# State-space stage of a four-layer kernel: another order of the engines' jobs, the first row's softplus sums and skip inputs dealt out, the bias prepared ahead

## The reference

```python
x = x + mamba(layernorm(x))      # the state-space stage: the change is here
x = x + experts(layernorm(x))    # 8 experts, the best 2 for each token, capacity 80 a row
x = x + attention(layernorm(x))  # causal, one head
x = x + experts(layernorm(x))
```

```python
xc, z = split(x @ in_proj_w + in_proj_b)
xc = silu(conv4(xc) + conv_b)                      # causal, per channel
delta_s, B, u = split(xc @ x_proj_w + x_proj_b)    # 16, 16, 512
delta = softplus(delta_s @ dt_proj_w + dt_proj_b)
h[t] = exp(-delta[t] * n) * h[t-1] + delta[t] * B[t, n] * u[t]    # n = 1..16
y = sum over n of h + u * D
out = (y * silu(z)) @ out_proj_w + out_proj_b
```

## Time and profile before

| | us |
|---|---|
| median of 3 runs | 2976.49 |
| the profiled execution | 2975.88 |
| its span | 2974.1 |
| first scan starts | 57.5 |
| last scan starts | 1620.0 |
| turn 1 (first scan of row 0 to that of row 1) | 97.3 |
| turn 2 | 97.0 |
| turns 3 to 14 | 98.2 to 99.4 |

### The profile page before, as it was taken

One profiled execution on the slowest core, in us unless ns is written; L12 is line 12 of the kernel. 1 busy time (PEld: TensorE's weight loads), 2 busy tenths in 40 slices (PEclk: granted clock), 3 DMA queues, 4 the chain that ended last, 5 costly groups with the idle time before them and its releaser, 6 DMA issues. The chain is left out here.

```text
span 2974.1 us, 48729 instructions
## 1 busy us (share of the span) xinstructions
PE 2760.2 (93%) x16944; PEld 2222.7 (75%) x16944; DVE 2274.6 (76%) x3610; ACT 1757.6 (59%) x3174; POOL 2190.4 (74%) x1437
## 2 busy tenths in 40 slices
PE   6999999999999899999986799999899997999998
PEld 3566656666666566656665799999898987999998
DVE  4898999999999998999888656565477775656564
ACT  4766776677667766776664445454366654544443
POOL 4889899899989999989987666666335557666664
PEclk9999999999999999999998899999999997999999
DMA  6132221122112211221125455545222234454542
GB/s 171 69 110 74 88 72 32 74 88 72 38 67 88 72 46 59 88 74 44 52 81 197 133 120 123 121 124 117 60 76 80 91 107 123 125 120 121 123 117 37
DMA packets 184191, 273.01 MB, mean 92 GB/s; under 512 B 35687, under 2 KB 156174, under 8 KB 175816
## 3 DMA queue, kind: packets, MB, share of 16 engines
q1 hardware_dynamic: 148680, 227.92, 23.2%
q0 software_dynamic: 35328, 42.76, 8.0%
HBM read 188.89 MB, written 94.72 MB: 95 GB/s over the span
## 5 line engine op out<-in xcount | busy, mean ns | idle before, releaser
L550 POOL TENSOR_TENSOR dbu<-du,bb 128x1024 f32<-128x1024 f32 x512 | 1196.8, 2365 | 27.4 <-DVE hs L703 24.2
L703 DVE TENSOR_TENSOR_SCAN hs<-da,dbu 128x1024 f32<-128x1024 f32 x512 | 1152.9, 2280 | 67.6 <-ACT da L638 29.0
L638 ACT ACTIVATE da<-delta 128x512 f32<-128x512 f32 x1024 | 567.9, 594 | 238.4 <-DVE hs L703 235.8
L808 PEld LDWEIGHTS yT<-ident,hs 128*128 128x128 f32 x4096 | 483.6, 146 | 142.3 <-issue 99.7
L808 PE MATMUL yT<-ident,hs 128*128 128x128 f32 x4096 | 540.2, 282 | 14.6 <-DVE hs L703 14.6
L1365 POOL TENSOR_TENSOR ffn_w_lo<-ffn_w,ffn_w_hi 128x512 fp32r<-128x512 f32 x240 | 320.7, 1339 | 80.3 <-ACT ffn_w_hi L1360 78.6
L1449 PE MATMUL ffn_hbank<-ffn_w_hi,ffn_hT_hi 128*128 128x256 f32 x1280 | 367.2, 287 | 0.3 <-DVE ffn_hT_lo L1436 0.3
L1451 PE MATMUL ffn_hbank<-ffn_w_hi,ffn_hT_lo 128*128 128x256 f32 x1280 | 360.2, 281 | 0.0
L1450 PE MATMUL ffn_hbank<-ffn_w_lo,ffn_hT_hi 128*128 128x256 f32 x1280 | 360.1, 281 | 0.0
L1414 PE MATMUL ffn_hbank<-ffn_rowsT_hi,ffn_w_hi 128*128 128x320 f32 x1024 | 318.5, 311 | 3.2 <-POOL ffn_w_lo L1365 3.2
L1415 PE MATMUL ffn_hbank<-ffn_rowsT_lo,ffn_w_hi 128*128 128x320 f32 x1024 | 318.1, 311 | 0.0
(11 more groups left out here) (260 smaller groups left out, 4957.3 us busy)
## 6 DMA issues: line engine op xcount, KB each, us to landing
bb<-b_rows SPq DMA_DIRECT2D x64, 1024.0 KB, 4.6
ffn_w<-L_ffn_W SPq DMA_DIRECT2D x60, 1024.0 KB, 6.2
slots<-empty SPq DMA_DIRECT2D x40, 530.0 KB, 8.2
empty<-slots SPq DMA_DIRECT2D x16, 662.5 KB, 4.9
ffn_rows<-slots SPq DMA_DIRECT2D x16, 662.5 KB, 4.8
xt<-L_attn_a_x SPq DMA_DIRECT2D x16, 512.0 KB, 3.9
x<-L_attn_a_x SPq DMA_DIRECT2D x16, 512.0 KB, 3.9
x_after_mamba<-x SPq DMA_DIRECT2D x16, 512.0 KB, 3.0
```

The lines of the kernel that those rows point to most:

```text
L550: pool.tensor_tensor(dbu[:, s % DEEP], du[:, dt, :].unsqueeze(1).to_broadcast([P, SN, T]), bb[:, q * SN:(q + 1) * SN, :], ALU.mult).then_i ...
L638: ins = act.activation(da[:, s % 2, i, :], delta[:, par, dt, :], ACT.Exp, scale=-float(q * SN + i + 1))
L703: dve.tensor_tensor_scan(flat[0], flat[1], flat[2], 0.0, ALU.mult, ALU.add).then_inc(scanned.sem, 1)
L808: mm = pe.matmul(yT[:, j * P:(j + 1) * P], hs[:, s % DEEP, i, j * P:(j + 1) * P], k.ident[:], start=False, stop=(q == QS - 1 and i == SN - ...
```

## The change

The job orders of all engines are written anew, and with them the step under which each job stands. The bank orders change too, so other pairs of jobs share a bank. Beside the order:

- log_part of row 0 is split: block 0 first, with a semaphore of its own (log_begun), then blocks 1 to 3. The softplus sums 1 to 3 of row 0, its step_input 1 and 2 and its skip_input 0 to 2 move from the end of turn 0 into the steps 0 to 5 of turn 1. The normalisation of row 1 moves from step 30 of turn 0 to step 1 of turn 1.
- stage_bias moves from step 0 of turn 1 to step 10 of turn 0.
- prompt_stats of the next row moves from step 13, behind gate 0, to step 12.
- route_place moves ahead of gate 2 in step 31.

```diff
-RING_JOBS = ("G3", "Z0", "U2", "O0", "T0", "T1", "U3", "I0", "I1", "O1", "G0", "Z1", "I2", "I3", "S", "RT0", "RT1",
-             "DA0", "DA1", "DA2", "DA3", "G1", "RL", "U0", "Z2", "U1", "G2", "RP", "Z3", "-")
+RING_JOBS = ("G3", "Z0", "U2", "O0", "T0", "T1", "U3", "I0", "O1", "I1", "G0", "I2", "Z1", "I3", "RT0", "S",
+             "RT1", "DA0", "DA1", "DA2", "DA3", "-", "RL", "G1", "U0", "Z2", "U1", "G2", "RP", "Z3")
...
         def softplus(pool, row, par, m):
-            pool.wait_ge(log_done.sem, log_done.at(row, 1))
+            if is_turn(row, 0) and m == 0:
+                pool.wait_ge(log_begun, 1)
+            else:
+                pool.wait_ge(log_done.sem, log_done.at(row, 1))
...
             act.wait_ge(exp_done.sem, exp_done.at(row, 2))
-            act.activation(tail_of_xc, tail_of_xc, ACT.Ln, bias=1.0).then_inc(log_done.sem, 1)
+            if is_turn(row, 0):
+                act.activation(tail_of_xc[:, 0, :], tail_of_xc[:, 0, :], ACT.Ln, bias=1.0).then_inc(log_begun, 1)
+                act.activation(tail_of_xc[:, 1:, :], tail_of_xc[:, 1:, :], ACT.Ln, bias=1.0).then_inc(log_done.sem, 1)
+            else:
+                act.activation(tail_of_xc, tail_of_xc, ACT.Ln, bias=1.0).then_inc(log_done.sem, 1)
... POOL
+                        if s == 1 and is_turn(turn, 1):
+                            softplus(pool, 0, 0, 1)
+                        if s == 3 and is_turn(turn, 1):
+                            softplus(pool, 0, 0, 2)
+                        if s == 5 and is_turn(turn, 1):
+                            softplus(pool, 0, 0, 3)
...
-                        if s == 30 and has_first(turn):
+                        if s == 27 and has_first(turn) and turn > 0:
                             softplus(pool, turn, par, 1)
+                        if s == 28 and has_first(turn) and turn > 0:
                             softplus(pool, turn, par, 2)
-                        if s == 31 and has_first(turn):
+                        if s == 30 and has_first(turn) and turn > 0:
                             softplus(pool, turn, par, 3)
... ACT
+                        if s == 0 and late:
+                            summed_copy(act, turn, turn - 2, 3)
                         if s == 1 and late:
                             gate_input(act, turn, 3)
-                            summed_copy(act, turn, turn - 2, 3)
...
-                        if s == 6 and first:
+                        if s == 4 and first:
                             for c in range(NC):
                                 turned(act, turn, par, c)
...
+                        if s == 26 and main:
+                            summed_copy(act, turn, row, 2)
+                        if s == 26 and first and turn > 0:
+                            skip_input(act, turn, turn, 0)
... DVE
-                        if s == 0 and is_turn(turn, 1):
-                            stage_bias(dve)
+                        if s == 1 and is_turn(turn, 1):
+                            step_input(dve, 0, 0, 0, 1)
...
-                        if s == 5 and main:
+                        if s == 6 and main:
                             step_input(dve, turn, row, 1 - par, 3)
                         if s == 10 and is_turn(turn, 0):
                             dve.wait_ge(loaded, 16 * CONSTS)
                             dve.tensor_tensor(b_skip[:], b_u[:], d_skip[:], ALU.mult).then_inc(skip_ready, 1)
                             dve.wait_ge(k.shaped, KIT_SHAPED)
+                            stage_bias(dve)
...
+                        if s == 12 and has_first(turn + 1):
+                            dve.wait_ge(x_ld.sem, x_ld.at(turn + 1, 16))
+                            prompt_stats(dve, norm, xt, turn + 1)
                         if s == 13 and main:
                             gate(dve, turn, 0)
-                        if s == 13 and has_first(turn + 1):
-                            dve.wait_ge(x_ld.sem, x_ld.at(turn + 1, 16))
-                            prompt_stats(dve, norm, xt, turn + 1)
                         if s == 13 and late:
                             route_stats(dve, turn, turn - 2)
...
-                        if s == 31 and first:
+                        if s == 29 and first and turn > 0:
                             step_input(dve, turn, turn, par, 1)
+                        if s == 31 and late:
+                            route_place(dve, turn, turn - 2)
                         if s == 31 and main:
                             gate(dve, turn, 2)
-                        if s == 31 and late:
-                            route_place(dve, turn, turn - 2)
... PE
                         if s == 3 and main:
                             x_proj(pe, turn, 3, 0)
+                        if s == 3 and first:
+                            in_proj(pe, turn, par, "I0", 0)
+                        if s == 4 and main:
                             x_proj(pe, turn, 3, 1)
...
                             dt_proj(pe, turn, 2)
-                        if s == 18 and first:
                             dt_proj(pe, turn, 3)
...
                             x_proj(pe, turn, 0, 0)
+                        if s == 23 and first:
                             x_proj(pe, turn, 0, 1)
...
-                        if s == 30 and main:
+                        if s == 31 and main:
                             in_proj(pe, turn, 1 - par, "Z3", ND + 3)
```

More of the change, by code:

```diff
@@ L972, in one_turn @@
                             summed_copy(act, turn, row, 0)
-                        if s == 9 and first:
+                        if s == 11 and first:
                             conv_input(act, turn, 1)
@@ L994, in one_turn @@
                             act.wait_ge(skip_ready, 1)
+                        if s == 19 and late:
+                            route_turned(act, turn, 1)
                         if s == 19 and main:
                             summed_copy(act, turn, row, 1)
-                        if s == 19 and first:
+                        if s == 20 and first:
                             delta_b(act, turn)
-                        if s == 19 and late:
-                            route_turned(act, turn, 1)
                         if s == 21 and first:
@@ L1118, in one_turn @@
                             pe.wait_ge(staged, STAGED)
+                        if s == 0 and late:
+                            out_proj(pe, turn, 0)
+                        if s == 1 and first:
+                            turn_x(pe, turn, 0)
                         if s == 1 and late:
-                            out_proj(pe, turn, 0)
                             out_proj(pe, turn, 1)
-                        if s == 2 and first:
-                            turn_x(pe, turn, 0)
                         if s == 3 and first:
@@ L1127, in one_turn @@
                             x_proj(pe, turn, 3, 0)
+                        if s == 3 and first:
+                            in_proj(pe, turn, par, "I0", 0)
+                        if s == 4 and main:
                             x_proj(pe, turn, 3, 1)
-                        if s == 4 and first:
-                            in_proj(pe, turn, par, "I0", 0)
-                        if s == 6 and first:
+                        if s == 6 and late:
+                            out_proj(pe, turn, 2)
@@ L1132, in one_turn @@
+                        if s == 7 and first:
                             in_proj(pe, turn, par, "I1", 1)
-                        if s == 7 and late:
-                            out_proj(pe, turn, 2)
                         if s == 8 and first:
                             conv_taps(pe, turn, 0)
-                            conv_taps(pe, turn, 1)
                         if s == 8 and late:
                             out_proj(pe, turn, 3)
+                        if s == 8 and first:
+                            conv_taps(pe, turn, 1)
@@ L1140, in one_turn @@
                         if s == 9 and main:
                             turn_back(pe, turn, row, 0)
+                        if s == 9 and first:
+                            in_proj(pe, turn, par, "I2", 2)
                         if s == 10 and main:
                             in_proj(pe, turn, 1 - par, "Z1", ND + 1)
-                        if s == 10 and first:
-                            in_proj(pe, turn, par, "I2", 2)
+                        if s == 11 and is_turn(turn, 0):
+                            pe.wait_ge(loaded, 16 * CONSTS)
@@ L1155, in one_turn @@
                             route_turn(pe, turn, turn - 2, 0)
-                        if s == 14 and late:
+                        if s == 13 and first:
+                            x_proj_small(pe, turn, 0)
+                        if s == 15 and late:
                             route_turn(pe, turn, turn - 2, 1)
```

94 lines of the change are left out of this document (50 added, 44 removed).

## The result

The kernel after takes 3013.35 us (median of 4 runs, 3012.37 to 3013.49) against 2975.59 of the kernel before: ratio 1.0124, 95% interval 1.0109 to 1.0139. It is slower, as forecast, but by 37.8 us and not by 21. The 2997 of the forecast was missed by 16 us, and the range, which ended at 3007, by 6.

The account below looks back on a forecast made before the run. Steady turns were taken as set by waits between engines, POOL pacing the first 29.3 us and DVE the rest. Terms -10.9 + 2 - 2.0 + 31.8 - 0.3 + 0.7 = +21.3 gave 2997 us; full range 2961 to 3007.

Parts of the forecast that it names:

- The sign and the first mechanism: Whole kernel slower, +21.3 us (slower 0.62): in steady turns norm_veps or norm_away loses the port until POOL's product 16 ends.
- Rival 1: Steady turns: norm_veps and norm_away both run between POOL products 15 and 16, +0.35 a turn; 2968 us, chance 0.22.
- rivals 2 and 4: 2: norm_veps' wait stays 0.4, turn gains 0.8, 2953, chance 0.07; 4: order costs nothing, start gives nothing, 2973, 0.08.
- The statistics of the next row: Turns 3 to 14: statistics at step 12 lose the port, scan 14 +2.95; with -0.3, +2.65 a turn, +31.8 in all.
- End of a turn: Steady turns, up to the routing's end: earlier yT copy and reordered gate 2, U0 and DA3; -0.3 a turn, bounds -1.0 to +1.0.
- The start: Row 0: split logarithm and U0's new bank bring the first scan from 57.52 to near 51.8; -5.7 us, bounds -1.5 to -6.5.
- The bias: Row 0: its DVE work between the first scans moves to idle time in turn 0; -6.2 us, 1 put back for softplus sums.
- the wait in turn 1: Turn 1: the same port wait costs about 3 us, of which 1 had been waited for anyway; +2 us.
- Turn 2: DVE's 3.06 us wait for U3 shrinks through earlier queueing and an earlier yT copy; -2.0 us, bounds 0 to -3.
- The tail: Turn 17: Z3 behind the last sum delays silu and gate 3 by 1.5, out_proj 2 gains 0.8; +0.7 us.
- Rival 3: Steady turns: scan 22 behind DA3, or xnT copies before decay 5, add 1 us each on top; +13, 3010 us, chance 0.08.

Follow-up runs that it names:

- kernel 2: Kernel after, with the next row's statistics put back behind gate 0 (step 13): 3003.84 us against 3023.75 for the kernel before, ratio 0.9945.
- kernel 1: Kernel before, with only the next row's statistics moved to step 12, ahead of gate 0: 3085.01 us against 3023.75, ratio 1.021.
- kernel 5: Kernel after, with the next row's statistics in step 13 but still ahead of gate 0: mean of turns 3 to 14 is 98.46 us (one run).
- the last kernel of part 7: Kernel after, with norm_veps and norm_away on POOL and Z3 at step 29, ahead of sum 30: 2961.14 us against 2976.72 for the kernel before.
- kernel 8: Kernel after, with norm_veps and norm_away on POOL and gate 0 in step 12 ahead of the statistics: 2946.91 us against 2976.77 for the kernel before.
- last kernel of part 5: Kernel after, with gate 0 moved to step 12, ahead of the statistics: 2989.40 us against 2976.77 for the kernel before, ratio 1.0040.

## Why the prediction was right and wrong

- *The sign and the first mechanism: right.* The place, step 12, and the way in which the port is lost were called: norm_veps in front of a boundary of queued products, ending only with product 16. It was norm_veps itself that lost it, so scan 14 came 2.75 us later, with 2.95 forecast. Rival 1 (slip through) is refuted in twelve turns of twelve; rivals 2 and 4 as well.
- *The step that failed: the term of "The statistics of the next row", +2.95 a turn, in which gate 0 costs its 0.6 us on DVE and the delay of scan 14 is taken for the delay of the turn.* The one move costs 4.06 a turn (kernel 2 against the kernel after), 1.1 more. The prediction moved gate 0 behind the wait and did not ask who waits for it: the bank of I3. PE then stands idle for 3.2 us and comes back at half clock, and from scan 14 to last_send it took 0.8 us more than before. Gate 0 early again, with the wait at the port kept, gives 1.93 us a turn back, 23 us in all. With the gate early the wait costs 2.13 and not 2.95, for scan 14 is then 2.2 us late; in the kernel after the rest of its 2.75 is gate 0's own 0.6 us. "End of a turn" (-0.3) was near: with the bank and job orders it gives -0.53. 12 x (4.06 - 0.53) = 42.4 against 31.8.
- *The start: right in place, and in size in this execution* (-6.3 for -5.7). PE's clock has a part in it. In the kernel before, U0 and U1 ran at a granted clock of 0.70 and the first scan came at 57.5; kernel 1, with the same start, had 0.83 there and 56.2. With the start of the kernel after, kernel 5, the last kernel of part 7 and kernel 8 have it at 54.0 to 54.1, with 5.6 to 5.8 us for the products of dt_proj that took 3.67 in the kernel after. The bias is as forecast: scan 1 of row 0 follows the first after 2.3 us in place of 8.5. The bias and the rest gave turn 1 -6.6 in kernel 2 (forecast about -5.2), and the wait in turn 1 took 4.6 of it back (forecast 2).
- *Turn 2: wrong* (+0.4 for -2.0). The gain for U3 is there: scan 3 to scan 6 takes 9.9 us in place of 12.7. But scan 1 came 2.0 us later, for silu 3 waits for a Z3 that stands behind the last sum, and the sums ahead of it ran below full clock. That this is the whole cause is not shown: with Z3 moved ahead it ran at half clock itself, and turn 2 did not get shorter.
- *The tail: mis-sized* (+4.0 for +0.7). Z3 behind the last sum was seen as 1.5 us less 0.8; PE came from an idle time and did it below full clock, and the first products of out_proj too (3.29 us for eight); out_proj starts 7.5 us behind the last scan in place of 4.1. How much of the 4.0 this is worth is not shown: kernels with the same tail differ by up to 2.9 us in the stretch to the expert phase.
- *Rival 3* (a later bound on top of the loss, 3010) was nearest in size, with another place: neither DA3 nor the xnT copies, but gate 0.

## What to carry to other kernels

When a job is moved on an in-order engine, list what then stands behind it and which buffer each of those jobs gives back, and to whom; a late consumer of a PSUM bank can cost as much as the wait itself, and the two prices need not add up. An idle stretch of PE on the path can cost twice, once as a wait and once as slow matmuls behind it. A small VectorE instruction that needs the shared port should not be placed in front of a queue of long POOL products: give it to POOL, or place it where POOL waits anyway.

## What the hardware showed

- A waiting TENSOR_SCALAR does not get the port at the next boundary when POOL has another product queued: arrived 0.9 us ahead of it, it took 3.27 us; 0.4 us ahead, 2.71 (last kernel of part 5); with POOL held for 0.18 us, 0.99. The subtraction of the bias, a TENSOR_TENSOR, did get in at a boundary (2.47 us); why the two differ is open. The Trainium skill, "SBUF — State Buffer", section "Who interferes with whom", gives the pair to whoever issues first; for norm_veps, issued before product 16, these rows differ, and the measurement decides.
- PE without work for 3.2 us came back at a granted clock of 0.57 over the next 4 us, and matmuls of 1.06 us in place of 0.59; after 1.07 us without work they took 0.59. The gap just ahead is not the whole of it: Z3 of the last kernel of part 7 ran at 0.57 with 0.76 us of idle time ahead, after 3.9 us at full clock in which PE was busy for 2.14.
